# A selective scan whose C rows come by DMA, and whose GpSimd B rows come through TensorE and ScalarE

## What is computed

```python
def step(h, inp):
    u_t, d_t, B_t, C_t = inp
    dA = jnp.exp(d_t[..., None] * As)
    h = h * dA + (d_t * u_t)[..., None] * B_t[:, :, None, :]
    y = jnp.einsum('bkcn,bkn->bkc', h, C_t)
    return (h, y)
h0 = jnp.zeros(u.shape[1:] + (As.shape[-1],), u.dtype)
_, ys = jax.lax.scan(step, h0, (u, d, Bt, Ct))
```

## Time and profile before

| what | us |
|---|---|
| median of three runs (2240.36 to 2246.75) | 2245.09 |
| span of the profiled execution | 2244.7 |
| scan stage: first input to last scan | 253.5 to 1409.1 |
| one tile, start to start | 96.4 |
| PE, DVE, ACT, POOL busy in the 96 us from 386 | 83.8, 94.5, 66.7, 94.7 |

### The profile page before, as it was taken

How to read it: one execution, slowest core, us unless ns; L and a number is a source line. 1 busy time by engine, 2 the same in 40 slices (tenths; PEclk the granted TensorE clock), 3 DMA queues, 4 the chain that set the end, 5 groups by cost and what they waited for, 6 DMA issues and landing times.

```text
span 2244.7 us, 20167 instructions
## 1 busy us (share of the span) xinstructions
PE 1984.1 (88%) x5826; PEld 919.6 (41%) x5830; DVE 1575.2 (70%) x1505; ACT 1144.9 (51%) x1258; POOL 1297.0 (58%) x464
## 2 busy tenths in 40 slices
PE   7988588888888888888888888989995999999997
PEld 3332133333333333333333333456653555555554
DVE  6978999999999999999999999774553000000000
ACT  4788666666776676776767666211213112122111
POOL 0110499999999999999999999401233011111110
PEclk9987599999999999999999999999997999999999
DMA  6448622233222233222232220611226233333300
GB/s 193 151 175 280 212 75 75 70 98 79 84 66 65 75 100 91 65 75 75 61 105 67 77 73 19 229 42 57 85 85 223 85 119 124 123 119 126 126 24 7
DMA packets 82402, 229.13 MB, mean 102 GB/s; under 512 B 14031, under 2 KB 40257, under 8 KB 80816
## 3 DMA queue, kind: packets, MB, share of 16 engines
q1 hardware_dynamic: 76208, 211.54, 29.6%
q0 software_dynamic: 6144, 16.98, 2.1%
HBM read 166.39 MB, written 64.03 MB: 103 GB/s over the span
## 4 chain that ended last, share of the span: by engine, by line
PE 46%; DVE 23%; issue 17%; POOL 8%; ACT 3%; DMA 1%; DVEq 0%; SPq 0%; ACTq 0%; POOLq 0%
DVE arena L1705 15%; PE ps L1489 11%; PE ps L1502 11%; PE ps L1229 6%; POOL arena L604 4%; POOL arena L587 4%; PE ps L1439 3%; PE ps L1213 2%; PE ps L1110 2%; DVE ps L1688 1%; PE ps L1226 1%; PE ps L1139 1%; PE ps L1390 1%; PE ps L1428 1%; DVE arena L1572 1%
## 5 line engine op out<-in xcount | busy, mean ns | idle before, releaser
L604 POOL TENSOR_TENSOR arena<-arena 128x2048 f32<-128x2048 f32 x192 | 868.3, 4533 | 16.6 <-DVE arena L1705 15.7
L1229 PE MATMUL ps<-arena 128*128 128x512 f32 x1536 | 727.7, 596 | 27.7 <-POOL arena L604 27.6
L1705 DVE TENSOR_TENSOR_SCAN arena<-arena,ps 128x1024 f32<-128x1024 f32 x264 | 587.5, 2266 | 0.0
L880 ACT ACTIVATE arena<-ps 128x1024 f32<-128x1024 f32 x384 | 390.7, 1017 | 248.0 <-PE ps L1213 246.1
L1213 PE MATMUL ps<-arena 96*128 (+1 forms) x1296 | 366.7, 384 | 129.3 <-DVE arena L1705 112.7
L1229 PEld LDWEIGHTS ps<-arena 128*128 128x128 f32 x1536 | 288.4, 190 | 287.7 <-issue 194.0
L587 POOL TENSOR_TENSOR arena<-arena 128x1024 f32<-128x1024 f32 x120 | 283.1, 2359 | 103.5 <-DMA arena<-b_rows 103.5
L2066 DVE TENSOR_TENSOR arena<-ps,arena 128x384 f32<-128x384 f32 x32 | 17.8, 557 | 450.4 <-PE ps L1502 450.4
L1688 DVE TENSOR_TENSOR ps<-ps,arena 128x1024 f32<-128x1024 f32 x264 | 309.1, 1216 | 12.6 <-PE ps L1213 12.6
L873 ACT ACTIVATE arena<-arena 128x1024 f32<-128x1024 f32 x264 | 300.8, 1139 | 8.9 <-DVE arena L1705 8.3
L1213 PEld LDWEIGHTS ps<-arena 96*128 96x128 bf16 x1296 | 112.9, 98 | 461.3 <-DVE arena L1705 215.7
(11 more groups left out here) (225 smaller groups left out, 1611.9 us busy)
## 6 DMA issues: line engine op xcount, KB each, us to landing
arena<-b_rows SPq DMA_DIRECT2D x240, 256.0 KB, 4.2
arena<-in_w SPq DMA_DIRECT2D x16, 2304.0 KB, 13.3
delta<-arena SPq DMA_DIRECT2D x24, 512.0 KB, 2.9
delta_x<-arena SPq DMA_DIRECT2D x24, 512.0 KB, 3.1
arena<-delta SPq DMA_DIRECT2D x24, 512.0 KB, 3.6
arena<-delta_x SPq DMA_DIRECT2D x24, 512.0 KB, 4.6
slot_in<-arena SPq DMA_DIRECT2D x8, 772.0 KB, 8.1
arena<-slot_in SPq DMA_DIRECT2D x8, 772.0 KB, 18.0
```

Source lines behind the costliest of these rows:

```text
L604: nc.gpsimd.tensor_tensor(hst[:, h:h + 2], hst[:, h:h + 2], c_sb[:, c:c + 2], ALU.mult).then_inc(p2_ok, 2)
L880: nc.scalar.activation(c_sb[:, u % RING], C_PS, ACT.Copy).then_inc(c_free, 1)
L1229: mm = pe.matmul(Y_PS[:, h * 512:(h + 1) * 512], ident, hst[:, u % HRING, h * 512:(h + 1) * 512], start=False, stop=(u == UN - 1))
L1705: nc.vector.tensor_tensor_scan(h, f, x, 0.0, ALU.mult, ALU.add).then_inc(sc_ok, 1)
```

## The change

C rows no longer pass through TensorE and ScalarE. They are kept in f32 in DRAM (`c_rows`, in the place of `b_rows`), and SyncE spreads them into `c_sb` by DMA, two units (two adjacent rows, 8 KB a partition) a transfer, one transfer for each half of 64 partitions. The B rows of the ten GpSimd units go the way that C went: TensorE spreads them into the bank pair that C had (now `BX_PS`), ScalarE copies them to `xin`. The bf16 parts hold only B.

```diff
+C_AT = 20
+ROWS_AHEAD = 2
...
-            def b_row(q, u):
...
+            def c_rows(U):
+
+                q, u = divmod(U, UN)
                 dr, n = divmod(u, N)
...
+                slot = U % RING
+                if U >= RING:
+                    sp.wait_ge(p2_ok, U + 2)
                 for im in range(2):
...
+                    at = im * N + n
+                    sp.dma_start(c_sb[H2 * im:H2 * im + H2, slot:slot + 2].rearrange("p u s -> p (u s)"),
+                                 row_dram[q // J, dr, at:at + 2].rearrange("n s -> (n s)").partition_broadcast(H2)).then_inc(c_ld[slot // 2], 16)
...
-                if U % UN in POOL_UNITS and U > POOL_UNITS[XRING - 1]:
-                    b_row(U // UN, U % UN)
+                if U % 2 == 0 and U >= C_AT:
+                    c_rows(U - C_AT + RING)
...
-                pool.wait_ge(b_ld[x % XRING], q * (32 * len(POOL_UNITS) // XRING) + 32 * (x // XRING + 1))
+                pool.wait_ge(bx_cp, q * len(POOL_UNITS) + (x + 1))
...
-                    pool.wait_ge(c_free, U + 3)
                     h, c = u % HRING, u % RING
+                    pool.wait_ge(c_ld[c // 2], q * (32 * UN // RING) + 32 * (u // RING + 1))
...
+            def pool_rows(q, x, fresh):
+                act.wait_ge(bx_ok, q * len(POOL_UNITS) + (x + 1))
+                if not fresh:
+                    old = POOL_UNITS[(x - XRING) % len(POOL_UNITS)] - (UN if x < XRING else 0)
+                    act.wait_ge(sc_ok, q * UN + (old + 3))
+                    settled(act)
+                nc.scalar.activation(xin[:, x % XRING], BX_PS, ACT.Copy).then_inc(bx_cp, 1)
...
-                    nc.scalar.activation(c_sb[:, u % RING], C_PS, ACT.Copy).then_inc(c_free, 1)
+                    if u % GROUP == 1 and u // GROUP < len(POOL_UNITS):
+                        x = u // GROUP + ROWS_AHEAD
+                        if x < len(POOL_UNITS):
+                            pool_rows(q, x, first and x < XRING)
+                        elif not last:
+                            pool_rows(q + 1, x - len(POOL_UNITS), False)
...
+            def pool_spread(q, x):
+
+                if x or not isinstance(q, int) or q:
+
+                    pe.wait_ge(bx_cp, q * len(POOL_UNITS) + x)
+                spread(q, POOL_UNITS[x], BX_PS).then_inc(bx_ok, 1)
...
-                        spread(q, u, 0, B_PS[u % 2]).then_inc(b_ok, 1)
+                        spread(q, u, B_PS[u % 2]).then_inc(b_ok, 1)
+                    if at == 0 and u // GROUP < len(POOL_UNITS):
+                        x = u // GROUP + ROWS_AHEAD
+                        if x < len(POOL_UNITS):
+                            pool_spread(q, x)
+                        elif not last:
+                            pool_spread(q + 1, x - len(POOL_UNITS))
                     if at == 1:
                         add_trailing_y(q, u - 1, first)
-                    pe.wait_ge(c_free, U + 1)
-                    spread(q, u, 1, C_PS).then_inc(c_ok, 1)
```

More of the change, by code:

```diff
@@ L112 @@
 K_ORDER = (0, 2, 1, 3)
-FIRST_DELTAS_AT, ROWS_EARLY = HALVES - 3, 2
+FIRST_DELTAS_AT = HALVES - 3
 def half_of(p, i):
@@ L193, in hybrid_block_kernel @@
         rb = Region(arena, XY, BCD)
-        bc = rb.take(2, 2, 2, S, dtype=BF16)
+        bc = rb.take(2, 2, S, dtype=BF16)
         dlt, dux = rb.take(2, S), rb.take(2, S)
@@ L296, in hybrid_block_kernel @@
         B_PS = [pair_of_banks(0), pair_of_banks(2)]
-        C_PS, Y_PS = pair_of_banks(4), pair_of_banks(6)
+        BX_PS, Y_PS = pair_of_banks(4), pair_of_banks(6)
         OP_PAIR, OP_BACK, OP_SEEN = (2, 4, 6, 4), (8, 4, 8, 4), 8
@@ L332, in hybrid_block_kernel @@
         rows_ok, rows_st, in_ok = sem("rows_copied"), [sem("rows_stored0"), sem("rows_stored1")], sem("input_on_pool")
-        b_ld = [sem(f"b_row{i}") for i in range(XRING)]
+        bx_ok, bx_cp = sem("pool_b_spread"), sem("pool_b_copied")
+        c_ld = [sem(f"c_rows{i}") for i in range(RING // 2)]
         dt_ok, d_ok, du_ok = sem("dt_filled"), sem("delta_ready"), sem("delta_x_ready")
-        b_ok, c_ok, c_free, dec_ok = (sem(n) for n in ("b_spread", "c_spread", "c_copied", "decay_ready"))
+        b_ok, dec_ok = (sem(n) for n in ("b_spread", "decay_ready"))
         p1_ok, sc_ok, p2_ok, ya_ok, yev_ok = (sem(n) for n in ("input_ready", "scanned", "readout_ready", "y_added", "y_evacuated"))
@@ L369, in hybrid_block_kernel @@
         LD_C = 16 * (len(CONSTS) + 1 + K)
[L370 removed]
+        PLACED = 16 * PART
         block = ctx.enter_context(nc.Block())
@@ L410, in store_parts @@
                     for dr in range(2):
-                        for m in range(2):
-                            lo = H2 * dr + m * SR
-                            sp.dma_start(bc_dram[x, part * SR:part * SR + SR, dr, m], parts[lo:lo + SR, o, part]).then_inc(bc_st[o], 16)
+                        lo = H2 * dr
+                        sp.dma_start(bc_dram[x, part * SR:part * SR + SR, dr], parts[lo:lo + SR, o, part]).then_inc(bc_st[o], 16)
                 sp.wait_ge(hi_ok, 2 * x + 1)
                 for dr in range(2):
-                    sp.dma_start(b_dram[x, dr], b_full[H2 * dr:H2 * dr + SR]).then_inc(rows_st[o], 16)
+                    sp.dma_start(row_dram[x, dr], b_full[H2 * dr + SR:H2 * dr + 2 * SR]).then_inc(rows_st[o], 16)
             def store_delta(p, i):
@@ L474, in _ @@
                             sp.wait_ge(z_st[j], 32 * NP)
-                        for u in POOL_UNITS[:ROWS_EARLY]:
-                            b_row(0, u)
-            for u in POOL_UNITS[ROWS_EARLY:XRING]:
-                b_row(0, u)
+            for k in range(2):
+                sp.wait_ge(bc_st[k], K * NP // 2 * PLACED)
+            c_rows(0)
+            c_rows(2)
             for i in range(MADE):
                 sp.wait_ge(dm_st[i], NP * HALVES // MADE * 32)
+            c_rows(4)
+            c_rows(6)
             sp.dma_start(w_out, a["w_out"]).then_inc(ld4, 16)
@@ L489, in _ @@
                     load_delta(half // 2, half % 2)
-                if U % UN in POOL_UNITS and U > POOL_UNITS[XRING - 1]:
-                    b_row(U // UN, U % UN)
+                if U % 2 == 0 and U >= C_AT:
+                    c_rows(U - C_AT + RING)
                 if U % (J * UN) == N and J * UN <= U < 3 * J * UN:
-                    sp.wait_ge(c_ok, U - N)
+                    sp.wait_ge(b_ok, U // UN * VEC_UNITS)
                     load_bc(U // (J * UN) + 1)
+            for U in range(NQ * UN - C_AT + RING, NQ * UN, 2):
+                c_rows(U)
             def load_z(c):
@@ L746, in split_hi @@
                 slot = fill_slot("xa", p, o)
-                nc.scalar.activation(b_full[0:H2 + SR], slot[0:H2 + SR], ACT.Copy).then_inc(hi_ok, 1)
+                nc.scalar.activation(b_full, slot, ACT.Copy).then_inc(hi_ok, 1)
                 nc.scalar.activation(parts[:, o, 0], slot, ACT.Copy).then_inc(hi_ok, 1)
@@ L888, in _ @@
             skip_weights(0)
+            for x in range(ROWS_AHEAD):
+                pool_rows(0, x, True)
             units(0, True, False)
@@ L1206, in _, with spread @@
                         x_proj("xd", *DT_ROWS_AT[p, s])
-            def spread(q, u, m, dst):
+            def spread(q, u, dst):
                 dr, n = divmod(u, N)
@@ L1213, in spread @@
                     mm = pe.matmul(dst[:, h * 512:(h + 1) * 512], sel_lhs[0:BR, n],
-                                   bc[0:BR, q % OJ // J, dr, m, h * 512:(h + 1) * 512], start=True, stop=True)
+                                   bc[0:BR, q % OJ // J, dr, h * 512:(h + 1) * 512], start=True, stop=True)
                 return mm
@@ L1263, in _ @@
             pe.wait_ge(dtev_ok, NP * HALVES)
+            pool_spread(0, 0)
+            pool_spread(0, 1)
             tile_steps(0, True, False)
```

21 lines of the change are left out of this document (3 added, 18 removed).

## The result

The changed kernel takes **2291.97 us** (median of four runs, 2284.69 to 2303.13), the kernel before 2243.83 beside it (2240.36 to 2246.75): a ratio of 1.0223, with a 95% interval of 1.0188 to 1.0258. It is slower by 48 us, and the forecast was 2275 in a range of 2250 to 2305. The profiled execution is one of the faster of the four: 2285.99 us, its span 2284.2, where the span before was 2244.7. So the trace holds 39.5 of the 48 us.

What follows compares the result with a forecast made beforehand. The bound was taken to be a loop through VectorE and GpSimd, 96.40 us a tile. 2245.09 + 25.4 for late C rows + 5 for TensorE's clock gave about 2275 us, range 2250 to 2305.

Steps and rivals of the forecast that it cites:

- The loop: Chain through VectorE and GpSimd around one tile: 56.92 + 7.50 + 29.52 + 2.46 = 96.40 us, becoming 88.47 + d.
- d: Time from the end of scan 15 until the C rows of unit 16 have landed: 10.2 us, +2.27 a tile.
- The cheap end: Low value for d: `delta_x` landed at 5.0, then 1.05 MB at 324 GB/s, 8.3 us; total 2250 us.
- the case of rows in time: Rival: C rows nearly or wholly in time for the readout of unit 16, 2240 to 2252 us; chance 0.15.
- Parts 1 and 2 at nothing: Relieving TensorE and ScalarE, and B rows of GpSimd's inputs through ScalarE: cost 0; only 0.43 us leaves the handover.
- The clock: TensorE at half clock after the late readout of unit 16: 0 to 2.15 us a tile, 0.5 taken, +5 in all.
- The rival of a clock that falls there: TensorE's clock also halves in the handover, 5.9 us more in half of the tiles: 2302 us; chance 0.12.
- Tile 11 at nothing: Last tile: handover gives back 0.43, first readout 1.4 us late, mostly covered by 1.19 of slack: 0.
- Tile 0 at +2.7: First tile: its own late readout of unit 16, 10.2 - 7.50 = +2.7 us.
- the first rows at nothing: First C rows queue behind the last stores ahead of the scan: 0, at most 2.3 us.
- The DMA queue as the bound: Rival: C rows below 191 GB/s make the queue set the tile, 102 us at 185: 2309 us; chance 0.07.
- The relieved engines: Rival: TensorE and ScalarE were the bound; handover wait of 1.52 goes, tile near 95.0: 2230 us; chance 0.04.

Runs made afterwards that it cites:

- the run over 128 partitions: The changed kernel with one C-row transfer over all 128 partitions for a pair of units in place of two over 64: 2261.54 us, ratio 1.0079.
- the kernel with even spreads: The changed kernel, list order kept (`C_AT` 20), with two extra TensorE spreads a group placed evenly: 2279.18 us, ratio 1.0156.
- the kernel with all three edits: The changed kernel with `C_AT` 16, evenly placed extra spreads, and the add of unit 0 behind the B spreads of units 6 and 7: 2234.07 us.
- The late add: The kernel before the change, with only the add of unit 0 moved behind the B spreads of units 6 and 7: 2232.52 us, ratio 0.9940.
- bursts ahead of B spreads: The changed kernel with each spread of GpSimd's B rows written three times: 2300.30 us with `C_AT` 20, 2256.28 us with 16.

## Why the prediction was right, and where its sizes were off

The direction was right, and the mechanism: the time is inside the range, 17 us above the value. Of these 17, 9 are in the span of the profiled execution (39.5 against 30.4), and 6 lie between this execution and the median of the four runs, which goes with the clock; the rest is mostly the 1.8 us of this execution outside its span, where the working reckoned with 0.4. Step by step:

- **The loop** held: 96.40 as a chain of four links, of which the changed kernel moved the ones named. From R16 to the end of R24 is still 29.4, from there to input 30 2.51, input 6 still waits 1.10, the 0.42 of scan 5 is gone. With the measured d the formula gives 88.47 + 10.5 = 98.97 for a tile; the tiles 5 to 8 have 98.94. One premise was taken without a row for it: that a late B spread of unit 30 holds VectorE up in full. The earlier trace rows show no wait at input 30. The changed kernel bears it out: R16 came 3.0 us later, and the tile grew by 2.55 and the 0.42 that left the handover.
- **d** was 10.2, from the landing of B rows behind the same load. In the tiles 5 to 8 it is 10.4 to 10.65 from the end of scan 15 to the start of R16, of which 0.13 lie between landing and start, which the step left out. A tile cost 2.55 in place of 2.27: 2.8 us in ten. The cheap end (8.3) and the case of rows in time needed a faster transfer; the run over 128 partitions shows that the form of the transfer decides most of it.
- **Parts 1 and 2 at nothing** held as far as TensorE's and ScalarE's time go: no wait stands at the GpSimd inputs but the first, and none for a decay but scan 5's 1.4 in the tiles 4 and 10. That the work taken off TensorE had a use, to hold the clock, is in the clock's term.
- **The clock** was mis-sized: 5 us, where the profiled run has some 7.5 in the tiles 1 to 10 (the 8.7 above less the 1.4 of later rows), and the median some 13, by the kernel with even spreads. It was a quarter of a bound, a guess, and the chosen range was wide enough for it. The place was right for the stretch behind the late R16, and that one is indeed free. What the step missed is that the clock falls in other places as well, with the rows in time too, at the handover among others. The rival of a clock that falls there came true in the tiles 4 and 10 alone, and cost scan 5 1.40 us each, not 5.9; the low stretch covers the adds ahead of the evacuation, not the whole chain.
- **Tile 11 at nothing** was wrong by 1.2. R0 was taken to be 1.4 late, by the d of R16. It stood 2.19 (962.12, above), and R2 another 0.27; R8's slack of 1.19 covers half of that, and in the last tile no late load hides the rest. Tile 0 at +2.7, and the first rows at nothing, were 2.9 together; the part behind the scan, +1.1, was not in the sum, and no run shows its cause.
- **Rivals.** The DMA queue as the bound fell, at 195 to 204 GB/s and up to 0.87 of its engines' time, with no wait but for the first rows, once these stood ahead of the load. The relieved engines were not the bound, though the 95.0 a tile that this rival named as GpSimd's floor is where the kernel with all three edits stands (95.0 to 95.2). The late add shows what kept the loop above it: the 1.10 at the handover, which this change leaves in place.

## What to carry to other kernels

When a transfer moves into an issuing engine's list, look for the wait that stands ahead of it there and for the bytes that this wait lets go first; its cost is the landing behind both, less the time at which the data are wanted, and one number that sets the list position took all of it back here. Work that is taken off an engine beside the path is not free if it kept that engine's clock up. Filler can bring the level back, but it must not stand ahead of work that the path waits for: here single spreads in the gaps cost nothing that shows, and bursts ahead of B spreads cost more than the clock gave back (with the rows ahead, 11 us). And before relieving two engines that have idle time, read which wait the loop closes on: moving one add behind two spreads, in the kernel as it was, took 0.6% off, and the whole change added 2.2%.
